# Second layer of a two-layer transformer kernel: its attention steps taken two at a time, the products with values between their transposes

## What is computed

```python
# attention of the second layer: 8 heads of 64, keys and values from a latent of 64
q = (x @ Wq.T); kv_latent = x @ Wkv_down.T
k = kv_latent @ Wk_up.T; v = kv_latent @ Wv_up.T
attn = softmax(q @ k.T / 8); out = (attn @ v) @ Wo.T
# and its second part, again an attention: 8 heads of 64, values mixed from 5 experts,
# two chosen for each token and head, and the output gated the same way
scores = (x @ Wq) / 8 @ (x @ Wk).T
probs = softmax(scores); attn = probs @ v
out = einsum('bthe,bthk,ekd->btd', mask_o, attn, Wo)
x = x + out                      # after each of the two; a layer norm stands ahead of each
```

## Time and profile before

| | |
|---|---|
| median of 3 runs | 2932.53 us (2927.82 to 2939.71) |
| the profiled execution, its span | 2945.6 us |
| TensorE busy (all stages) | 2437.2 us, 83% |
| VectorE, ScalarE, GpSimd busy | 65%, 57%, 65% |
| mean granted TensorE clock | 0.883 of full |
| stage three | from about 1600 us to the end |

### The profile page before, as it was taken

One profiled execution on the slowest core, in us unless ns is written; L12 is line 12 of the kernel. 1 busy time (PEld: TensorE's weight loads), 2 busy tenths in 40 slices (PEclk: granted clock), 3 DMA queues, 4 the chain that ended last, 5 costly groups with the idle time before them and its releaser, 6 DMA issues. The chain is left out here.

```text
span 2945.6 us, 31726 instructions
## 1 busy us (share of the span) xinstructions
PE 2437.2 (83%) x10259; PEld 1143.9 (39%) x10259; DVE 1901.8 (65%) x3077; ACT 1690.7 (57%) x2384; POOL 1929.2 (65%) x1920
## 2 busy tenths in 40 slices
PE   5667777777877777764988999999999999999995
PEld 2222323332323232232555444444444444444442
DVE  4798989898979897821333564656556564656554
ACT  0678888888888889920221545454444544454351
POOL 5455587877777778856775018575657475764776
PEclk8668787878787877776999999999999999999998
DMA  2000000000100000163996000000000100000000
GB/s 99 6 9 1 17 15 17 15 17 15 15 17 15 17 8 17 17 111 66 284 268 154 14 1 1 1 15 8 15 8 1 22 1 22 1 8 1 8 1 14
DMA packets 92452, 98.99 MB, mean 34 GB/s; under 512 B 20320, under 2 KB 88032, under 8 KB 92256
## 3 DMA queue, kind: packets, MB, share of 16 engines
q1 hardware_dynamic: 66544, 69.80, 8.9%
q0 software_dynamic: 25712, 26.90, 4.7%
HBM read 69.98 MB, written 26.67 MB: 33 GB/s over the span
## 5 line engine op out<-in xcount | busy, mean ns | idle before, releaser
L948 POOL TENSOR_TENSOR TT<-TT,SS 128x512 f32<-128x512 f32 x512 | 651.9, 1309 | 216.3 <-ACT SS L877 215.8
L1648 ACT ACTIVATE PR<-S,NM 128x512 f32<-128x512 f32 x512 | 347.6, 684 | 492.5 <-DVE NM L1816 492.3
L1816 DVE TENSOR_REDUCE NM<-S 128x2 f32<-128x1024 f32 x256 | 313.1, 1223 | 293.0 <-PE S L1552 292.2
L700 DVE TENSOR_SCALAR TT<-SC 128x1024 f32<-128x1024 f32 x256 | 311.7, 1218 | 80.2 <-POOL TT L948 44.7
L447 PE MATMUL OB<-TT,VAL 128*17 128x512 f32 x1024 | 343.8, 774 | 4.8 <-ACT TT L885 4.8
L953 POOL DMA_INDIRECT slot_tokens<-TID,IDX x256 | 260.0, 1016 | 130.6 <-issue 79.6
L702 DVE SCALAR_TENSOR_TENSOR SS<-SC,TT 128x1024 f32<-128x1024 f32 x256 | 313.6, 1225 | 20.6 <-issue 1.8
L1581 PE MATMUL OT<-TT,VN 128*64 128x512 f32 x1024 | 278.3, 622 | 20.5 <-ACT TT L1654 16.7
L1552 PE MATMUL S<-TT 64*128 64x512 f32 x1024 | 292.1, 646 | 0.7 <-ACT TT L1617 0.7
L1563 PEld LDWEIGHTS TP<-ident,PR 128*128 128x128 f32 x2048 | 226.9, 141 | 149.7 <-issue 121.0
L1563 PE MATMUL TP<-ident,PR 128*128 128x128 f32 x2048 | 275.4, 277 | 10.1 <-DVE TT L1821 8.7
(11 more groups left out here) (272 smaller groups left out, 4168.6 us busy)
## 6 DMA issues: line engine op xcount, KB each, us to landing
TT<-w_gu SPq DMA_DIRECT2D x64, 384.0 KB
TT<-w_dn SPq DMA_DIRECT2D x64, 128.0 KB
XL<-x SPq DMA_DIRECT2D x8, 512.0 KB
rows<-XL SPq DMA_DIRECT2D x8, 512.0 KB
slot_tokens<-TID,IDX POOLq DMA_INDIRECT x256
TT<-w_dn SPq DMA_DIRECT2D x64, 64.0 KB
XS<-stream SPq DMA_DIRECT2D x8, 512.0 KB, 3.8
out<-XS SPq DMA_DIRECT2D x8, 512.0 KB, 2.9
```

What stands on the lines that cost most here:

```text
L700: dve.tensor_scalar(tt[:, :, mt, :], SC[mt % 2][:], 0.0, None, ALU.max)
L948: ins = pool.tensor_tensor(tt, tt, ss, ALU.add)
L1648: act.activation(PR[s % 2][h2][:], S[s % 2][:, h2, :], ACT.Exp, bias=NM[:, s % 2, h2:h2 + 1], accum_out=SM[:, pair % 2, j, h2:h2 + 1]).the ...
L1816: dve.tensor_reduce(NM[:, s % 2, :], S[s % 2][:], AX, ALU.max, negate=True).then_inc(sems["peak"], 1)
```

## The change

All loops of stage three take two steps at a time (`twos`). On TensorE a pair of steps s, s+1 is: turn s; items of step s in slots 1 and 2; both products with values of the pair before; turn s+1; items of step s+1 in slot 1; the scores of s+2 and s+3; then the rest of the items. ScalarE and VectorE follow the same order. `spread` uses transposes. `attend` has its wait for copies only in the tail (`last`).

```diff
+    def twos():
+        for r in range(TAIL):
+            for s in range(0, STEPS, 2):
+                yield r, s
...
             def spread(v, pair, b):
...
-                    ins = pe.matmul(bank[:, j * P:(j + 1) * P],
-                                    RB[:, 2 * j:2 * j + 2, :].rearrange("p h d -> p (h d)"), ident[:], start=True, stop=True)
+                    ins = pe.transpose(bank[:, j * P:(j + 1) * P],
+                                       RB[:, 2 * j:2 * j + 2, :].rearrange("p h d -> p (h d)"), ident[:])
...
-            def attend(v, r, pair, m):
+            def attend(v, r, pair, m, last):
...
-                    for way in "da":
-                        if v.all_due("in_" + way):
-                            pe.wait_ge(sems["in_" + way], v.value)
+                    if last:
+                        for way in "da":
+                            if v.all_due("in_" + way):
+                                pe.wait_ge(sems["in_" + way], v.value)
...
+            for r, s in twos():
+                turn(v, r, s)
+                carry(v, parts, r, s, 1, 2)
                 rr, pair = behind(r, s)
+                if rr >= 0:
+                    attend(v, rr, pair, s % NT, False)
+                    attend(v, rr, pair, s % NT + 1, False)
+                turn(v, r, s + 1)
+                carry(v, parts, r, s + 1, 1)
+                for at in (ahead(r, s), ahead(r, s + 1)):
+                    if at:
+                        scores(v, *at)
+                carry(v, parts, r, s, 3, 4)
+                carry(v, parts, r, s + 1, 2, 3, 4)
+            for s in range(NT + 1):
+                carry(v, parts, TAIL, s, 1)
+                if s < NT:
+                    attend(v, TAIL - 1, PAIRS1 - 1, s, True)
+                carry(v, parts, TAIL, s, 2, 3, 4)
```

ScalarE's loop after:

```diff
+            for r, s in twos():
+                turned(v, r, s)
+                carry(v, parts, r, s, 1, 2)
+                turned(v, r, s + 1)
+                carry(v, parts, r, s + 1, 1)
+                for at in (ahead(r, s), ahead(r, s + 1)):
+                    if at:
+                        numerators(v, *at)
+                carry(v, parts, r, s, 3, 4)
+                carry(v, parts, r, s + 1, 2, 3, 4)
```

VectorE's loop after:

```diff
+            for r, s in twos():
+                turned(v, r, s)
+                carry(v, parts, r, s, 1, 2)
+                turned(v, r, s + 1)
+                carry(v, parts, r, s + 1, 1)
+                for at in (ahead(r, s), ahead(r, s + 1)):
+                    if at:
+                        peak(v, *at)
                 rr, pair = behind(r, s)
+                if s % NT == 0 and rr >= 0:
                     shares(v, rr, pair)
+                carry(v, parts, r, s, 3, 4)
+                carry(v, parts, r, s + 1, 2, 3, 4)
```

More of the change, by code:

```diff
@@ L1598, in _ @@
             scores(v, 0, 1)
[L1599 to L1604, removed]
-                rr, pair = behind(r, s)
-                if rr >= 0 and rr < TAIL and (r < TAIL or s < NT):
-                    attend(v, rr, pair, s % NT)
-                carry(v, parts, r, s, 2, 3, 4)
+            for r, s in twos():
+                turn(v, r, s)
+                carry(v, parts, r, s, 1, 2)
+                rr, pair = behind(r, s)
+                if rr >= 0:
[13 more added lines that the diff above has]
+                carry(v, parts, TAIL, s, 2, 3, 4)
         @block.scalar
@@ L1679, in _ @@
             numerators(v, 0, 1)
[L1680 to L1686, removed]
+            for r, s in twos():
[8 more added lines that the diff above has]
+                carry(v, parts, r, s + 1, 2, 3, 4)
+            for s in range(NT + 1):
+                carry(v, parts, TAIL, s, 1, 2, 3, 4)
         @block.vector
@@ L1863, in _ @@
             peak(v, 0, 1)
[L1864 to L1869, removed]
+            for r, s in twos():
[6 more added lines that the diff above has]
+                        peak(v, *at)
                 rr, pair = behind(r, s)
-                if s % NT == 1 and 0 <= rr < TAIL:
+                if s % NT == 0 and rr >= 0:
                     shares(v, rr, pair)
-                carry(v, parts, r, s, 2, 3, 4)
+                carry(v, parts, r, s, 3, 4)
+                carry(v, parts, r, s + 1, 2, 3, 4)
+            for s in range(NT + 1):
+                carry(v, parts, TAIL, s, 1)
+                if s == 1:
+                    shares(v, TAIL - 1, PAIRS1 - 1)
+                carry(v, parts, TAIL, s, 2, 3, 4)
         @block.gpsimd
```

## The result

The changed kernel took 3105.11 us (median of 4 runs, 3102.44 to 3109.36) against 2931.15 us for the kernel before (4 runs): a ratio of 1.0575, 95% interval 1.055 to 1.060. That is 174 us more, where 124 were forecast (3057 us, range 2975 to 3165).

A forecast was written before the change was run, and what follows sets the result against it. TensorE's own work was taken to bound stage three. Added costs of 174 us, less 19 (wait), 16 (spread) and some 15 (GpSimd), gave + 124 on the median of 2932.5: 3057 us, range 2975 to 3165.

The forecast's parts named there:

- only the scores of s+3 lie between: Between scores of s+2 and their turn, about 4 us of TensorE's work shrinks to these scores, exposing softmax latency 128 times.
- The opening of stage three: Existing scores-scores-turn sequence taken as sample: turn starts 3.26 us after the scores, with 1.28 us idle for ScalarE's exponential.
- The pair without items: Two steps of stage three carrying no items: 7.32 us instead of 6.18, 1.14 us more, saving of 0.35 inside.
- Cover of slot 2: Items in slot 2 of odd steps fill the gap, up to 1.5 us each: 6.2 us less per two runs.
- The bank and ScalarE's copies: Neighbouring slots 1 and 2 in even steps wait for bank BK, 5.6 us; late ScalarE copies, 4.2 us, per two runs.
- The dropped wait: TensorE's wait for copies out of TP before products with values goes: 19 us less, nothing taking its place.
- Spread: Four products of 0.99 us become four transposes of 0.49, 32 times: 16 us less.
- whatever shortens TensorE's stream is gained in full: In stage three, where TensorE stands at 9 tenths, any work taken off it should shorten the time by as much.
- GpSimd's waits: TensorE's waits for GpSimd's work, 18 us: some 15 us less, as that work comes relatively sooner when TensorE is slower.
- The clock: Rival, chance 0.16: TensorE's clock falls to half in a third of the 128 pairs, 99 us more, 3156 us.
- the forecast's sum before its deductions: Stage three's added cost, 21.8 us per two runs, eight times: 174 us, before savings were taken off.
- The rival "faster": Rival, chance 0.05: exponentials of s+2 come in time, so savings of 45 + 16 + 19 = 80 us remain, 2852 us.

The follow-up runs named there:

- c2_cover: Changed kernel with both products with values moved behind the scores of s+2 and s+3, on TensorE alone: 2950.22 us, ratio 1.0045 to the kernel before.
- b2_short: Changed kernel with the maximum over 64 of the 512 keys and queries scaled down by 50, for timing only: 3004.73 us, ratio 1.0229 to the kernel before.
- c1_filled: Changed kernel with one more unread full-width product ahead of the exponential's wait in each even step's turn: 3112.16 us, ratio 1.0595 to the kernel before.
- b4_slot2: Changed kernel with slot 2 items of even steps moved behind the products with values, on TensorE: 3040.36 us, ratio 1.0356 to the kernel before.
- a2_wait: Kernel before, without the products' wait for the copies of the last turn: 2926.58 us, ratio 0.9965.
- a1_spread: Kernel before, with only spread done by transposes: 2929.5 us, ratio 0.9972.
- a4_three: Kernel before with spread by transposes, the wait dropped and both products with values together, scores left in place: 2917.07 us, ratio 0.9931.
- c6_slot2: c2_cover with slot 2 items of even steps behind the scores, readers between the two steps' exponentials and maxima: 2964.83 us, ratio 1.0098 to the kernel before.

## Why the prediction was right, and where it was off

**Direction and cause: right, and shown.** The step "only the scores of s+3 lie between" carried the sum. Three runs point at it from different sides: cover moved into the gap gives back 155 us (c2_cover), a shorter maximum 101 us (b2_short, against 33 in the order before), filler costs about 7 (c1_filled). The first two move other waits too, so they bound the chain's share and don't measure it alone. The opening of stage three was a good sample: 3.26 us there, 3.35 in the run of it; 1.28 idle there, 1.37 here.

**The pair without items:** 7.47 instead of 7.32 us, 128 x 0.15 = up to 19 us too little; less where items cover. Of the 0.15, 0.06 is the turn: in the earlier trace rows a product of full width follows it, in the pair the tiled products with values, and so the change of shape was left out.

**Cover of slot 2:** 92 waits were left of 128; five covered pairs in sixteen, as the timetable was read, leave 88.

**The bank and ScalarE's copies:** charged at 78 us. The bank's waits rose by 66, and b4_slot2 took 65 us off. Right within a fifth, if each is taken for the whole. Its lower bound of nothing was wrong: the waits don't hide in one another. The row forecast as "the bank's waits grown by 40 to 50 us" grew by more, 66.

**The dropped wait, 19 us:** its waits are gone from the changed kernel, but as a saving against the kernel before it was mis-sized: alone it gives 10 (a2_wait), as the wait for OT's reader, at most 0.8 us each, takes its place. The prediction had written "Nothing takes its place", which is wrong in the old order.

**Spread, 16 us:** the group nearly halved as read, the time fell by 8 (a1_spread). So "whatever shortens TensorE's stream is gained in full" is not borne out by it. The Trainium skill's four times (TensorE: Matmul & The Clock Gate, section Terms) is not borne out against these products with the identity: 0.99 to 0.53 us.

**GpSimd's waits: the step that failed in sign.** I took off 15 of 18 us. The wait for GO did go (10.0), but that for the norm went from 8.0 us (two waits, which I read as one) to 29.3: 7.2 and 7.1 at two places and 2.4 to 2.6 at each of six. `stats` stands in slot 3 of an even step, now behind two maxima and all of the odd step's first slot, and its consumer `turn_norm` did not move. VectorE's timeline in the changed kernel shows it: the last output product is added, then come a copy and both maxima, and only then the norm's sums.

```profile
2424.43 0.42 DVE L1756 TENSOR_TENSOR XS<-XS,BK 128x256 f32<-128x256 f32 x1 [1.47 <-PE BK L1495]
...
2428.39 2.36 DVE L1836 TENSOR_REDUCE NM<-S 128x2 f32<-128x1024 f32 x2 [0.81 <-PE S L1557]
2430.66 1.40 DVE L1732 BATCH_NORM_STATS2 statl<-XS 128x6 f32<-128x256 f32 x4
```

GpSimd then needs until 2438.97 us, and TensorE has waited 2.5 us for it. Together 26 us mis-sized. That place I had named only for `choose`.

**The clock:** a rival with its own price, not a term of the forecast. It came in part, 58 us more at half level. TensorE's work takes twice as long there, so up to 29 us of the 50 that are missing. The cause I gave (the gap in pairs without cover) does not hold, as c1_filled and c2_cover show; most falls stand at the starts of latent runs and at the norm's waits, where several waits follow each other. What each fall cost was not measured separately: no run here changed the clock alone.

As a check, the stage's account, an estimate from one profile of each kernel: waits + 169, second halves of turns 92 x 0.21 = + 19, clock up to + 29, saved shapes and spread - 45 and - 16: + 156 of 173 us. The rest, some 17 us, stays open; some 6 of it may be that a gap from start to start (3.35 less the 1.92 of the scores) is 0.06 us longer than the view of waits says. That the measured 174 us equals the forecast's sum before its deductions is chance: the terms above are off in both directions.

**The rival "faster":** its price was too high also in its own terms. With the scores' place kept, the other three parts give 20 us (a4_three) and not 54, since other waits take over: OT's reader and the copies, with the clock longer at half. c2_cover and c6_slot2 group everything by shape and still lose by 0.5 and 1.0%. The best version found is a4_three, 0.7% under the kernel before.

## What to carry to other kernels

When steps are grouped to save the engine's changes of shape, first write down for each producer what the bounding engine still does before its consumer comes: here the grouping saved 0.35 us a pair and took some 3 us of cover from a chain of 3.3. Put the work that depends on nothing recent (here the products with values of the pair before) behind the start of the chain, and don't let two users of a single bank become neighbours. A saving read off one group is an upper bound: here spread gave 8 of 16 us, the dropped wait 10 of 19 and three parts together 20 of 54, while the products with values alone cost 21. For the dropped wait the reason is on record: the next wait in line stood at most 0.8 us behind.

## What was not expected of the hardware

A product of full width put ahead of the exponentials' wait 127 times, 92 of them with about 1.4 us idle, cost some 7 us in all and did not hold the clock: 15 falls against 18. And stretches in which a third of TensorE's time is transposes kept the full clock before (around the place of the earlier trace rows it was 1.00 too). The Trainium skill (TensorE: Matmul & The Clock Gate, Part 4) says that transposes don't count as busy time for the clock in the same way; in this case that can't be told from products making up the rest.
